# Three second-head slopes of a graph-attention layer: from VectorE to a ReLU on ScalarE and an accumulating DMA

## The reference

```python
h = (x @ W).reshape(n, H, C)
s_src = (h * a_src).sum(-1)
s_dst = (h * a_dst).sum(-1)
e = jax.nn.leaky_relu(s_src[src] + s_dst[dst], 0.2)
emax = jax.ops.segment_max(e, dst, num_segments=n)
ee = jnp.exp(e - emax[dst])
denom = jax.ops.segment_sum(ee, dst, num_segments=n)
alpha = ee / denom[dst]
out = jax.ops.segment_sum(alpha[:, :, None] * h[src], dst, num_segments=n)
```

## Time and profile before

| | us |
|---|---|
| median of 3 runs | 955.05 (953.85 to 957.43) |
| the profiled execution | 955.21 |
| its span | 953.5 |
| TensorE busy | 914.1 (96%) |
| VectorE busy | 747.3 (78%) |
| ScalarE busy | 351.7 (37%) |
| POOL busy | 134.5 (14%) |
| mean DMA rate | 172 GB/s |

### The profile page before, as it was taken

The page is one execution under the profiler, slowest core; times in us unless marked ns, Lnnn a source line. Parts: engine busy times, 40 slices in busy tenths (PEclk is TensorE's granted clock), DMA queues, the critical chain, the costliest instruction groups (busy, mean ns, idle before and its releaser), DMA issues.

```text
span 953.5 us, 17420 instructions
## 1 busy us (share of the span) xinstructions
PE 914.1 (96%) x6466; PEld 673.5 (71%) x6466; DVE 747.3 (78%) x1710; ACT 351.7 (37%) x466; POOL 134.5 (14%) x153
## 2 busy tenths in 40 slices
PE   6999999999999999999999999999998799999996
PEld 6867676766665565557699999779867566666663
DVE  7978999997877799897899998698989644445453
ACT  5751212122336223324445544265547232323230
POOL 3400000000002000000000000020010345454532
PEclk9999999999999999999999999999999999999998
DMA  9621212147367789678793100159495778778870
GB/s 324 193 66 32 70 64 70 68 145 272 117 217 210 235 243 281 204 233 288 251 335 126 56 1 1 34 120 306 192 346 199 262 197 186 201 172 203 190 175 9
DMA packets 78844, 164.29 MB, mean 172 GB/s; under 512 B 28308, under 2 KB 47638, under 8 KB 75818
## 3 DMA queue, kind: packets, MB, share of 16 engines
q1 hardware_dynamic: 63402, 117.18, 35.8%
q0 software_dynamic: 10944, 38.22, 16.6%
q10 hardware_dynamic: 4416, 7.78, 2.2%
HBM read 109.13 MB, written 50.51 MB: 167 GB/s over the span
## 4 chain that ended last, share of the span: by engine, by line
PE 70%; DVE 19%; DMA 4%; issue 3%; ACT 2%; SPq 1%; DVEq 0%; POOL 0%; POOLq 0%; ACTq 0%
PE PS L2080 45%; PE PS L2363 15%; PE PS L2187 3%; DVE arena L1802 3%; PE PS L2566 2%; DVE arena L1619 2%; DVE arena L1625 1%; DVE arena L1440 1%; PE PS L2198 1%; DMA arena<-in_L_ffn_W_dram 1%; PE PS L2581 1%; DVE arena L1602 1%; DMA arena<-g_d 1%; PE PS L2259 1%; PE PS L2272 1%
## 5 line engine op out<-in xcount | busy, mean ns | idle before, releaser
L2080 PE MATMUL PS<-arena 128*128 128x384 f16 (+7 forms) x3396 | 556.8, 319 | 5.3 <-DVE arena L1440 1.2
L2080 PEld LDWEIGHTS PS<-arena 128*128 128x128 f16 (+2 forms) x3396 | 318.2, 98 | 208.7 <-DVE arena L1680 4.0
L2363 PE MATMUL PS<-arena 128*128 128x193 f32 (+1 forms) x1200 | 178.7, 311 | 4.0 <-DVE arena L1625 2.9
L2363 PEld LDWEIGHTS PS<-arena 128*128 128x128 f32 x1200 | 176.3, 191 | 6.6 <-DVE arena L1625 3.8
L1204 ACT ACTIVATE arena<-arena,AS 128x1250 f32<-128x1250 f32 x60 | 80.0, 1338 | 72.5 <-DVE arena L1619 71.8
L1625 DVE SCALAR_TENSOR_TENSOR arena<-arena 128x1250 f32<-128x1250 f32 x60 | 87.2, 1454 | 5.7 <-PE PS L2363 5.6
L1505 DVE TENSOR_SCALAR arena<-arena 128x240 f16<-128x240 f16 x324 | 88.4, 273 | 0.0
L1619 DVE SCALAR_TENSOR_TENSOR arena<-arena,AS 128x1250 f32<-128x1250 f32 x55 | 83.0, 1510 | 0.0
L1504 DVE TENSOR_SCALAR arena<-arena 128x128 f16<-128x128 f16 x324 | 79.5, 245 | 0.1
L2069 DVE SCALAR_TENSOR_TENSOR arena<-PS,arena 128x768 f32<-128x768 f32 x25 | 23.9, 958 | 57.8 <-PE PS L2080 57.8
L1329 ACT ACTIVATE arena<-PS 128x1536 f16<-128x1536 f16 x27 | 39.2, 1451 | 74.7 <-PE PS L2566 74.7
(11 more groups left out here) (280 smaller groups left out, 931.6 us busy)
## 6 DMA issues: line engine op xcount, KB each, us to landing
arena<-in_L_ffn_W_dram SPq DMA_DIRECT2D x48, 384.0 KB, 3.9
fr_d<-arena SPq DMA_DIRECT2D x48, 384.0 KB, 3.3
arena<-fr_d SPq DMA_DIRECT2D x16, 1152.0 KB, 12.4
arena<-in_x_dram SPq DMA_DIRECT2D x18, 384.0 KB, 5.6
arena<-rr_d SPq DMA_DIRECT2D x4, 1280.0 KB, 8.7
g_d<-arena SPq DMA_DIRECT2D x10, 388.0 KB, 2.5
acc_d<-arena SPq DMA_DIRECT2D x10, 384.0 KB, 3.8
xf_d<-arena ACTq DMA_DIRECT2D x10, 384.0 KB, 3.1
```

The source lines that it names most:

```text
L2080: m = T.matmul(out, left[i][x], right[i][y], start=first and i + r == 0, stop=last and 3 * i + r == n - 1)
L2363: m = T.matmul(ps[sum_bank(h, b)][:, r * (C + 1):(r + 1) * (C + 1)], (PT1 if deep == 3 else PT)[i % deep][:, d * P:(d + 1) * P], feats, st ...
```

## The change

The second head's units 11, 14 and 17 get their slopes as the five in the first head do. `RELU` grows by these three; `RELU0` is the number in the first head. TensorE makes the row of second-head destination logits in three pieces (one per PSUM bank) in place of 22 warm-up products, ScalarE copies them, scaled by 0.8, to AD81 after the first exponential. The ReLUs (`relu1`) stand on ScalarE behind units 8, 9 and 10, the accumulating DMAs on POOL behind the two sums in HBM. The places that they write are RR's two rows of head 0 and unit 7's. They share the semaphores of the first three, so these are waited for at 32 and the experts' gather semaphores of the end count from ZROWS = 32. VectorE's slopes run up to two units ahead from unit 1 on. Semaphore counts follow: s_row_psum has three increments more, s_row_ready six.

```diff
-                return zsum[RELU.index(unit - U0)]
+                return zsums[RELU.index(unit - U0)]
...
+        zsums = [*zsum, RR[:, 0, 0, 0:N], RR[:, 0, 1, 0:N], zsum[3]]
+        AD81 = reg(20224 + 2 * D + 2 * N, NP)[:, 0:N]
...
-        RELU = (0, 2, 5, 7, 9)
+        RELU = (0, 2, 5, 7, 9, 11, 14, 17)
+        RELU0 = sum(1 for u in RELU if u < NT)
...
         ZADDS = 16
+        ZROWS = 32
...
 # SyncE
             sp.wait_ge(late_sums, 16 * len(LATER))
-            sp.wait_ge(s_p_ready, U0 + RELU[-1] + 1)
+            sp.wait_ge(s_p_ready, U0 + NT)
+            sp.wait_ge(s_row_ready, 11)
             for u in summed:
                 experts(u)
...
 # GpSimd
-            for k in range(len(RELU)):
+            for k in range(RELU0):
                 g.dma_start(zsum[k], RR[:, 0, 1, 0:N], accum_op=ALU.add).then_inc(z_in[k], 16)
             pool.wait_ge(xa_out[1], XAS)
             for b, t in enumerate(LATER):
                 pool.wait_ge(s_late_ready, 2 * (b + 1))
                 g.dma_start(acc_d[t * P:(t + 1) * P, :], LATE[:, b, :], accum_op=ALU.add).then_inc(late_sums, 16)
+            for k in range(RELU0, len(RELU)):
+                pool.wait_ge(s_row_ready, 9 + k - RELU0)
+                g.dma_start(zsums[k], RR[:, 1, 1, 0:N], accum_op=ALU.add).then_inc(z_in[k - RELU0], 16)
             pool.wait_ge(s_t2_ready, U0 + sloped_before(NT))
-            pool.wait_ge(s_p_ready, U0 + RELU[-1] + 1)
+            pool.wait_ge(s_p_ready, U0 + RELU[RELU0] + 1)
...
 # ScalarE
                 if i in RELU:
-                    act.wait_ge(z_in[RELU.index(i)], 16)
+                    k = RELU.index(i)
+                    if k < RELU0:
+                        act.wait_ge(z_in[k], 16)
+                    else:
+                        act.wait_ge(z_in[k - RELU0], ZROWS)
...
-                    act.wait_ge(s_row_psum, 3 + k + 1)
+                    act.wait_ge(s_row_psum, 3 + k + 1 if k < 2 else 7 + k)
...
+                def relu1(k):
+                    i = RELU[k]
+                    if k == RELU0:
+                        act.wait_ge(s_t2_ready, U0 + sloped_before(NT))
+                    elif k == RELU0 + 2:
+                        act.wait_ge(s_p_ready, U0 + RELU[3] + 1)
+                    a.activation(zsums[k], AD81, ACT.Relu, bias=AS8[:, 1, i - NT:i - NT + 1]).then_inc(s_row_ready, 1)
...
                     expo(H1 * NT + i, h, t)
+                    if i == 0:
+                        act.wait_ge(s_max_done, (H1 + H2) * NT)
+                        for n, (c0, w) in enumerate(CH):
+                            act.wait_ge(s_row_psum, 5 + n + 1)
+                            c1 = min(c0 + w, N)
+                            a.activation(AD81[:, c0:c1], PS[:, 5 * 512 + c0:5 * 512 + c1], ACT.Copy, scale=1.0 - SLOPE).then_inc(s_row_ready, 1)
                     if i in (1, 3):
                         row_out(2 + i // 2)
+                    if i in (8, 9, 10):
+                        relu1(RELU0 + i - 8)
...
 # VectorE
                     k = SLOPED.index(unit - U0)
+                    if k == 1:
+                        dve.wait_ge(s_row_psum, 8)
...
-                    while ahead < len(SLOPED) and SLOPED[ahead] <= i + (2 if 0 < i < NT else 1):
+                    while ahead < len(SLOPED) and SLOPED[ahead] <= i + (2 if i else 1):
                         if SLOPED[ahead] == NT:
-                            dve.wait_ge(s_row_ready, 5)
+                            dve.wait_ge(s_row_ready, 8)
...
 # TensorE
-                            pe.wait_ge(s_row_ready, 5)
+                            pe.wait_ge(s_row_ready, 8)
...
                 if k:
-                    pe.wait_ge(s_row_ready, 1 + k)
+                    pe.wait_ge(s_row_ready, (0, 2, 4, 7)[k])
                 for t in range(NT):
+                    if k == 2 and t in (4, 8):
+                        pe.wait_ge(s_row_ready, 4 + t // 4)
...
-            pe.wait_ge(s_late_ready, 3)
-            keep_warm(22, 4)
+            pe.wait_ge(s_row_ready, 3)
+            for c0, w in CH:
+                T.matmul(PS[:, 5 * 512 + c0:5 * 512 + c0 + w], a2c[:, 1, 1:2].to_broadcast([KS, P]), h2T[:, NP + c0:NP + c0 + w], start=True, stop=True).then_inc(s_row_psum, 1)
             row(2)
...
-                pe.wait_ge(rows_back[i % 3], ZADDS + 16 * (i // 3 + 1))
+                pe.wait_ge(rows_back[i % 3], ZROWS + 16 * (i // 3 + 1))
```

More of the change, by code:

```diff
@@ L607, in gps_layer @@
         ZADDS = 16
-        assert RELU[-1] < NT
+        ZROWS = 32
+        assert RELU0 == len(zsum) and RELU[RELU0 - 1] == NT - 1 and len(RELU) == RELU0 + len(rows_back)
         def sloped_before(i):
```

## The result

The changed kernel takes 962.15 us (median of 7), the kernel before 955.08 beside it: a ratio of 1.0072, 95% interval 1.0049 to 1.0095. The prediction said 957.4, 952.4 to 960.8. The profiled execution took 962.15; its span is 960.4 against 953.5.

The account below looks back on a forecast made before the run. TensorE carries 70% of the chain but waits for VectorE in layer 2's second head, 4.5 us winnable. Opening 0, units with the late DMA +1.7 and clock +0.6 made +2.3 us: 957.4 us, range 952.4 to 960.8.

Parts of the forecast that it names:

- E11: ScalarE's exponential of unit 11, in layer 2's second head; said to wait for its slope's DMA until 668.8.
- the opening: Start of layer 2, where products and three scaled copies replace warm-up; claimed cost 0, under 1.7 us at the copies' upper bound.
- Z11: First of the three new accumulating DMAs, for unit 11's slope; landing taken as 668.8 (bounds 668.1 to 671.3), making +1.7 us.
- the walk: Unit-by-unit timing through layer 2: -2.7 us if every exponential is on time, +1.7 with the DMA landing at 668.8.
- The clock: TensorE's clock falling after an idle from 667.2 to 671.7 in layer 2; +0.6 us, bounds 0 and 1.2.
- A19: TensorE's aggregation of unit 19, the last of layer 2; said to end at 694.5 against 692.8, without the clock's term.
- A10: TensorE's aggregation of unit 10, first of the second head; said to end at 667.2, ahead of TensorE's idle.
- A11: TensorE's aggregation of unit 11; said to start at 671.7, 3.2 us later than before, after TensorE's idle.
- shared from the start, and cold: Third rival: Z11 lands at 671.3 (+4.3), Z14 at 677.2, full 1.2 us of clock: +5.5, 960.6; chance 0.20.
- Z14: Accumulating DMA for unit 14's slope; said to land at 674.4, 5.6 us after Z11, hidden by 0.7 us.
- E14: ScalarE's exponential of unit 14, in the second head; its turn said to be 675.1, after Z14's landing.
- The first rival: On POOL's queue, Z11 doesn't wait for the late sums and lands at 662.4, or by 664.4: -2.7, 952.4; chance 0.13.

Follow-up runs that it names:

- units whose turn comes later: The changed kernel with units 14, 16 and 18 in place of 11, 14 and 17: 954.24 us against 956.71 before, ratio 0.9982.
- the second profile of the changed kernel: The changed kernel unaltered, timed again: 963.15 us, ratio 1.0055 to the kernel before.
- without the DMAs: The changed kernel without the second head's three accumulating DMAs, so it doesn't compute the layer: 953.1 us against 956.71 before, ratio 0.9953.
- the best: The changed kernel with masked experts held until unit 11's DMA lands, plus 11 more warm-up products among the logit columns: 954.58 us, ratio 0.9966 to before.
- the opening alone: The changed kernel's layer 2 opening with the old RELU, so no slope saved, no new ReLU or DMA: 955.09 us against 955.96 before, ratio 0.9994.
- row DMAs ahead of the sums: The changed kernel with POOL's three new accumulating DMAs ahead of the two late sums instead of behind them: 956.13 us, ratio 0.9985 to before.

## Why the prediction was wrong, point by point

- **The mechanism was right.** ScalarE stands at E11 for a DMA that was issued at 656.8 behind the two late sums, as said, and nothing of the rest costs: the opening (53.12 alone), the ReLUs and the traffic (53.13). The gain was open to the kernel only with the DMAs on time for their readers: with Z11 in 5.6 us after its issue the stretch is 3.3 us under the old one, and with units whose turn comes later it is 1.9 under.
- **The step that failed is the size of Z11's landing.** The prediction took 668.8, near its lower bound of 668.1, on the ground that SyncE's reads had not moved beside a full POOL queue. Z11 landed at 671.5, just past the upper bound of 671.3. Of the 2.7 us, 1.0 is that the second late sum landed at 666.4 and not at 665.4, as in the old kernel. The other 1.7 are in Z11's distance behind it, 5.2 us where 3.4 were taken. The ground held for the reads that went out at 666.4, which moved next to nothing until 670. It missed that the earlier experts' reads were still moving until 667, and it gave the new ones no part at the end. By the walk, 2.7 us later is 2.7 us more: +4.4 in place of +1.7. With the clock kept full the stretch is 3.9 us longer, which is this term as measured.
- **The clock was mis-sized, 0.6 for about 2.** I bounded it at 1.2, by a stretch with shorter gaps; here it was at half for some 10 us, 6.6 of them with matmuls. The Trainium skill (TensorE: Matmul & The Clock Gate, The HAM clock gate) says that an idle TensorE goes back to half rate, and the granted clock of 0.50 from 670 us agrees. By the walk the two terms together are 4.4 + 2.2 = 6.6 against 6.0 measured; the walk underrates the saved slopes by about the 0.6 between (3.3 against 2.7).
- **The miss in terms.** The forecast was 957.4, the time 962.15. Of the 4.8 us between, 2.2 are the landing (3.9 for 1.7), 1.6 the clock (2.2 for 0.6) and 0.9 lie behind A19.
- **A wait I didn't see.** I let A10 run to 667.2 and put the gap at A11. It is in A10, from 666.1 on, for PSUM banks 0 and 1. At full clock its last 8 matmuls would have fitted ahead of A11 anyway (673.4 to 674.3, and W11 ends at 674.4), so by this working it added under 1 us, and that only at half clock. No run takes this wait away by itself.
- **After A19** there are 0.9 us more. The kernels here have between 260.5 and 262.4 us from A19's end to the span's end, among them 262.3 in the second profile of the changed kernel, 260.8 without the DMAs and 262.4 in the best. I can't tell it from the executions' own spread, and it stays open. The 6.8 us at half clock near 750 us are not its cause by themselves: the opening alone has as much there and the shortest of these stretches, 260.5.
- **The rival that came true** is the third, "shared from the start, and cold", with +5.5 at a chance of 0.20. Z14 landed at 677.4, where it said 677.2, but E14 did not wait for it, since all that stands behind E11 came as late. The first rival, a queue that isn't one, did not come: wherever a trace here has the landings of POOL's late sums and new DMAs, they are in the order of issue. What it cites on completion the Trainium skill says of DMAs that SyncE and ScalarE issue. The Trainium skill's formula for a DMA's time (DMA: Bandwidth & Descriptors, Anatomy of one DMA), with its estimate of 3.5 us here, was off by 2 us even for one alone: 5.5 in the earlier trace rows, 5.6 with the masked experts held back.

## What to carry to other kernels

Work that moves from an engine to a DMA isn't priced by its size but by what is outstanding when it is issued: here 5.5 or 5.6 us for 625 KB into engines that are idle or nearly so, 10 to 12 behind another queue's reads, 14.7 behind two sums of its own queue and these reads. Put the landing, not the issue, against the turn of its reader, and look at all that stands behind that reader in the same stream: here one exponential held the scalings behind it, and the first four of these held all of TensorE. The spacing of one landing behind another can be read from the old trace, but it belongs to the load under which it was read: 5.2 to 6.0 us beside SyncE's reads, about 3 without them. Where the bounds give 668.1 to 671.3, ask which reads will be moving, the older ones too, and take the spacing of that case.

## What the runs showed of the hardware

- A queue that starts while the other's transfers are outstanding waited 3 to 5 us for its first packets: over 4 us for POOL's behind 5.9 MB of SyncE's (issued 657.99, 5 packets by 663), 3.8 us with the row DMAs ahead of the sums (issued 662.16, none from then until 666), about 5 us for SyncE's behind POOL's (issued 634.4, 3 packets by 640). After that they share by about halves: POOL's moves about 0.1 MB in a us, against 0.20 alone. Why the start takes so long no run shows.
- An accumulating DMA of 625 KB moves at 0.195 MB/us when POOL's queue is alone; SyncE's reads move at 0.44 MB/us when they are alone (row DMAs ahead, 662 to 664).
- Holding 3.5 MB of reads back by 23 to 25 us (the three masked experts, issued from 661.6 instead of 636.9) made the DMA that mattered land 9 us sooner after its issue. It cost the stretch nothing, and TensorE waits for the experts only beyond 750 us; behind A19 the three profiles of it have 260.7, 261.6 and 262.4 us, within what all the kernels have.
- TensorE's clock fell in a gap of 7.3 us and cost about 2 us behind it, as 60 products in the gap showed. At 610 us, among logit columns that change in no kernel but one, the profiles show between 0 and 13.7 us at 1.2 GHz, and A0 starts some 5 us later in the three that have most.
